# A graph network's first gather stage: transposes one slot ahead, a ring of ten slots, gathers unrolled

## What is computed

```
h    = concat([x[src], edge_attr], axis=1) @ W1 + b1      # 400000 x 64
mu, var = mean(h, axis=0), var(h, axis=0)                  # batch norm over all edges
msg  = silu((h - mu) * rsqrt(var + EPS) * g1 + be1)
agg  = segment_sum(msg, dst) / max(count(dst), 1)
```

## Time and profile before

| | |
|---|---|
| median of three runs | 10885.92 us (10885.71 to 10889.72) |
| the profiled execution's span, first to last instruction (no other time of it is given) | 10892.7 us |
| first gather stage, about 29 to 5072 us | 5043 us |
| between the gather stages | about 1150 us |
| second gather stage and the end | about 4670 us |
| busy share of the span: PE, DVE, ACT, POOL | 38%, 23%, 11%, 62% |
| granted TensorE clock, mean | 0.555 |

### The profile page before, as it was taken

How to read it: one execution, slowest core, us unless ns; L and a number is a source line. 1 busy time by engine, 2 the same in 40 slices (tenths; PEclk the granted TensorE clock), 3 DMA queues, 4 the chain that set the end, 5 groups by cost and what they waited for, 6 DMA issues and landing times. The chain is left out here.

```text
span 10892.7 us, 119855 instructions
## 1 busy us (share of the span) xinstructions
PE 4140.9 (38%) x36713; PEld 3322.5 (31%) x36713; DVE 2557.8 (23%) x7060; ACT 1173.7 (11%) x2055; POOL 6799.3 (62%) x6897
## 2 busy tenths in 40 slices
PE   4445444444444445445887311111111111111113
PEld 3333333333333333334776211111111111111112
DVE  2111111111111111114997311111111111111112
ACT  0000000000000000001334300000000000000001
POOL 5555555555555555556998466666666666666663
PEclk7655555656665655555555555555555555555555
DMA  2222222222222222222443111111111111111111
GB/s 78 60 61 61 61 61 60 61 61 61 61 61 61 61 60 61 61 61 75 125 123 114 50 44 44 43 45 44 44 44 44 44 43 45 44 43 45 44 44 35
DMA packets 882270, 637.83 MB, mean 59 GB/s; under 512 B 534579, under 2 KB 780831, under 8 KB 881496
## 3 DMA queue, kind: packets, MB, share of 16 engines
q1 hardware_dynamic: 590300, 326.49, 10.9%
q0 software_dynamic: 200416, 208.55, 10.2%
q10 hardware_dynamic: 91536, 102.58, 2.7%
HBM read 528.19 MB, written 108.90 MB: 58 GB/s over the span
## 5 line engine op out<-in xcount | busy, mean ns | idle before, releaser
L349 POOL DMA_INDIRECT Z<-in_x_dram,idx_ring x3125 | 2958.8, 947 | 2088.3 <-DVE idx_ring L526 1205.2
L1156 POOL DMA_INDIRECT X<-x_scratch,idx_ring x3125 | 2986.5, 956 | 1738.3 <-issue 893.5
L1185 PE MATMUL PS<-hot_c,msg_c 128*64 128x48 f32 x6250 | 811.6, 310 | 3865.8 <-ACT msg_c L1171 2630.0
L1185 PEld LDWEIGHTS PS<-hot_c,msg_c 128*64 128x64 f32 x6250 | 713.5, 223 | 3964.0 <-issue 2528.7
L401 PE MATMUL PS<-ZT,W_sb 128*64 128x256 f32 x2500 | 689.5, 647 | 2375.0 <-ACT ZT L451 2238.9
L515 DVE BATCH_NORM_STATS2 stats<-PS 128x320 f32 (+1 forms) x625 | 311.6, 499 | 3158.2 <-remote 2670.5
L1216 DVE TENSOR_TENSOR table<-table,PS 64x48 f32 x625 | 130.0, 208 | 3773.0 <-remote 1822.2
L401 PEld LDWEIGHTS PS<-ZT,W_sb 128*64 128x64 f32 x2500 | 183.7, 199 | 2637.2 <-ACT ZT L451 2488.9
L451 ACT ACTIVATE ZT<-PS 128x640 f32<-128x640 f32 x625 | 439.4, 703 | 4602.4 <-remote 4300.2
L391 PE MATMUL PS<-ident,Z 128*128 128x128 f32 x3125 | 845.7, 413 | 161.7 <-issue 158.6
L420 PE MATMUL PS<-W_sb,ZT 128*64 128x64 f32 x12500 | 877.7, 318 | 0.0
(11 more groups left out here) (140 smaller groups left out, 2682.9 us busy)
## 6 DMA issues: line engine op xcount, KB each, us to landing
Z<-in_edge_attr_dram SPq DMA_DIRECT2D x625, 160.0 KB
h_scratch<-h_ring ACTq DMA_DIRECT2D x625, 160.0 KB
h_turns<-h_scratch SPq DMA_DIRECT2D x125, 800.0 KB
E<-in_edge_attr_dram SPq DMA_DIRECT2D x625, 160.0 KB
Z<-in_x_dram,idx_ring POOLq DMA_INDIRECT x3125
X<-x_scratch,idx_ring POOLq DMA_INDIRECT x3125
x_nodes<-in_x_dram SPq DMA_DIRECT2D x1, 3125.0 KB
x_ring<-in_x_dram SPq DMA_DIRECT2D x25, 125.0 KB
```

The source lines that it names most:

```text
L349: nc.gpsimd.indirect_dma_start(out=Z[:, s, j, 0:D], out_offset=None, in_=x, in_offset=bass.IndirectOffsetOnAxis(ap=idx_ring[:, s, j:j + 1] ...
L1156: nc.gpsimd.indirect_dma_start(out=X[:, s, j, :], out_offset=None, in_=x1_dram, in_offset=bass.IndirectOffsetOnAxis(ap=idx_ring[:, s, j:j ...
L1185: last = nc.tensor.matmul(PS[D:P, s % 2, 0:WIN], msg[:, s, j, :], hot[:, s, j, :], start=(j == 0), stop=(j == TG - 1))
```

## The change

- PE transposes slot g+1 before the dense work of slot g. `ZT` has two buffers, taken by parity, so ACT's copy of slot g waits for the dense work of g-2.
- `Z`, `h_ring` and the one-hot have ten slots (RING = 2 S) in place of five. A turn has a half, 0 or 1, and the loops (`loop_halves`) run two turns a round.
- SP and POOL wait for the transposes of the slot ten back, with one counter `rows_done`. POOL's 3125 gathers are written out without a loop, and each takes its indices from a fixed column of `src_idx`; the copy into `idx_ring` (L526) and its signal are gone from this stage.
- DVE makes the one-hot of slot g+1 before it waits for slot g's results. ACT's store is that of two slots back.
- Several semaphores by slot become one counter each.

```diff
-            Z = sb(here, "Z", [P, S, TG, 2 * D])
-            ZT = sb(here, "ZT", [P, EG])
-            h_ring = sb(here, "h_ring", [P, S, TG, D])
+            RING = 2 * S
+            Z = sb(here, "Z", [P, RING, TG, 2 * D])
+            ZT = sb(here, "ZT", [P, 2, EG])
+            h_ring = sb(here, "h_ring", [P, RING, TG, D])
...
+            def later(i):
+                return not isinstance(i, int) or i >= 2
+
+            def next_slot(i, half, s, n):
+
+                return (i, half, s + 1, n) if s + 1 < S else (i + 1, 1 - half, 0, n + half)
...
+                            if later(i):
+                                sp.wait_ge(rows_done, i * S + (s + 1 - RING))
+                            sp.dma_start(Z[:, r, :, D:2 * D], edge_v[i * S + s]).then_inc(e_loaded[r], 16)
...
-                    def turn(i):
-                        for s in range(S):
-                            reuse(pool, idx_ready[s], i)
-                            reuse(pool, rows_done[s], i)
+                    for g in range(G):
+                        r = g % RING
+                        if g >= RING:
+                            pool.wait_ge(rows_done, g + 1 - RING)
                             carry_wait(pool)
-                            for j in range(TG):
-                                nc.gpsimd.indirect_dma_start(
-                                    out=Z[:, s, j, 0:D], out_offset=None, in_=x,
-                                    in_offset=bass.IndirectOffsetOnAxis(ap=idx_ring[:, s, j:j + 1], axis=0)
-                                ).then_inc(gathered[s], 16)
+                        for j in range(TG):
+                            n = g * TG + j
+                            nc.gpsimd.indirect_dma_start(
+                                out=Z[:, r, j, 0:D], out_offset=None, in_=x,
+                                in_offset=bass.IndirectOffsetOnAxis(ap=src_idx[:, n:n + 1], axis=0)
+                            ).then_inc(gathered[r], 16)
...
+                    def turn_rows(i, half, s, n):
+                        r = half * S + s
+                        if later(i) or i * S + s >= 2:
+                            pe.wait_ge(zt_taken, i * S + (s - 1))
+                        pe.wait_ge(e_loaded[r], n * 16 + 16)
+                        pe.wait_ge(gathered[r], n * (16 * TG) + 16 * TG)
...
+                        last.then_inc(rows_done, 1)
+
+                    def dense(i, half, s):
...
+                        pe.wait_ge(zt_taken, i * S + s + 1)
+                        if beyond:
+                            pe.wait_ge(count_added, i * S + (s - 1))
...
+                    def turn(i, half, n):
+                        for s in range(S):
+                            if not (isinstance(i, int) and i == SB - 1 and s == S - 1):
+                                turn_rows(*next_slot(i, half, s, n))
+                            dense(i, half, s)
...
+                            act.wait_ge(rows_done, i * S + s + 1)
+                            if later(i) or i * S + s >= 2:
+                                act.wait_ge(h_put, i * S + (s - 1))
+                            act.activation(ZT[:, two, :], banks(2 * two, 2, P, EG), ACT.Copy).then_inc(zt_taken, 1)
+                            if s >= 2:
+                                store(i, half, s - 2)
...
-                            nc.vector.tensor_copy(idx_ring[:, s, :],
-                                                  src_idx[:, ds(i * (S * TG) + (S + s) * TG, TG)]
-                                                  ).then_inc(idx_ready[s], 1)
+                            if not (isinstance(i, int) and i == SB - 1 and s == S - 1):
+                                one_hot(*next_slot(i, half, s, n))
+                            dve.wait_ge(ht_put, i * S + s + 1)
```

More of the change, by code:

```diff
@@ L313, in gnn_kernel @@
             h_put = sem("h_put")
-            h_ready = sems("h_ready")
-            h_stored = sems("h_stored")
+            h_ready = sem("h_ready")
+            h_stored = [sem(f"h_stored{r}") for r in range(RING)]
             stats_done = sem("stats_done")
@@ L379, in _ @@
                     pe.wait_ge(windows_ready, 1)
-                    def turn(i):
-                        for s in range(S):
[L383 to L418, removed]
-                                for lo in (0, D):
-                                    last = nc.tensor.matmul(PS[lo:lo + D, 6 + s % 2, j * D:(j + 1) * D],
-                                                            ZT[:, j * P + lo:j * P + lo + D], W1_sb[:, :],
-                                                            start=True, stop=True)
-                            last.then_inc(h_put, 1)
@@ L424, in _ @@
-                    turn(0)
-                    with pe.Fori(1, SB) as i:
-                        turn(i)
+                    def turn_rows(i, half, s, n):
+                        r = half * S + s
+                        if later(i) or i * S + s >= 2:
+                            pe.wait_ge(zt_taken, i * S + (s - 1))
+                        pe.wait_ge(e_loaded[r], n * 16 + 16)
+                        pe.wait_ge(gathered[r], n * (16 * TG) + 16 * TG)
+                        for j in range(TG):
+                            last = nc.tensor.transpose(banks(2 * (r % 2), 2, P, EG)[:, j * P:(j + 1) * P],
+                                                       Z[:, r, j, :], ident[:, :])
+                        last.then_inc(rows_done, 1)
@@ L457, in _, with store, turn @@
-                    turn(0)
-                    with act.Fori(1, SB) as i:
-                        turn(i)
-                    store(SB - 1, S - 1)
+                    def store(i, half, s):
+                        act.wait_ge(h_ready, i * S + s + 1)
+                        r = half * S + s
+                        act.dma_start(h_dram[i * S + s], h_ring[:, r, :, :].rearrange("p t c -> p (t c)")
+                                      ).then_inc(h_stored[r], 16)
+                    def turn(i, half, n):
+                        for s in range(S):
+                            two = (half * S + s) % 2
+                            act.wait_ge(rows_done, i * S + s + 1)
[4 more added lines that the diff above has]
+                                store(i, half, s - 2)
+                            elif not (isinstance(i, int) and i == 0):
+                                store(i - 1, 1 - half, s + S - 2)
@@ L530, in _ @@
-                    turn(0)
-                    with dve.Fori(1, SB) as i:
-                        turn(i)
+                            r = half * S + s
+                            two = r % 2
+                            if not (isinstance(i, int) and i == SB - 1 and s == S - 1):
+                                one_hot(*next_slot(i, half, s, n))
+                            dve.wait_ge(ht_put, i * S + s + 1)
+                            nc.vector.bn_stats(stats[:, ds(i * (6 * S) + 6 * s, 6)],
+                                               PS[:, 4 + two, 0:HC]).then_inc(stats_done, 1)
@@ new lines, in turn @@
+                            if not isinstance(i, int) or i * S + s > 0:
+                                dve.wait_ge(count_added, i * S + s)
+                            nc.vector.tensor_tensor(table[0:D, ds(firsts[s], WIN)], table[0:D, ds(firsts[s], WIN)],
+                                                    PS[0:D, 4 + two, HC:HC + WIN], ALU.add).then_inc(count_added, 1)
+                            dve.wait_ge(h_put, i * S + s + 1)
+                            if later(i):
+                                dve.wait_ge(h_stored[r], n * 16)
```

105 lines of the change are left out of this document (60 added, 45 removed).

## The result

The changed kernel took 10586.79 us (median of three runs, 10557.65 to 10588.93) against 10885.92 us: 0.9715 of the time before, 95% interval 0.9697 to 0.9732. That is 2.9% or 299 us faster. The forecast was 10452 us, 434 us faster. The profiled execution of after has a span of 10555.5 us and is the fastest of its three; that of before had 10892.7 us.

The account below looks back on a forecast made before the run. Gathers holding back TensorE's results, 1.41 to 1.43 us each, were taken as the bound. (8.05 - 7.35) x 620 slots = 434 us; 10892.7 - 434 - 7 = 10452 us; range 9960 to 10800 us, 8 times in 10.

Parts of the forecast that it names:

- Gathers hold back TensorE's results, 1.41 to 1.43 us each: Both gather stages: TensorE's results show late during gather trains, which makes 7.05 to 7.15 us a slot.
- The turn of 6.68 us: First gather stage: TensorE's time from one copy's end to the next copy, including some delay of the signal.
- The release: First gather stage: transposes of the slot ten back free gathers, so a train restarts about 3015.1 in place of 3016.03.
- The order on TensorE: First gather stage: transposing ahead takes the wait for the copy, 0.75 us a slot, off TensorE's path.
- slow bound: First gather stage: trains still of ten with the earlier restart, 7.63 us a slot.
- Trains longer than ten, with pauses left: First gather stage: 7.35 us a slot, taken between 7.1 and 7.63, saving 434 us over 620 slots.
- two bounds: First gather stage: quick bound 7.1 us a slot without pauses, slow bound 7.63 us with trains of ten.
- The start: Start of the first gather stage: the run-up's train of 50 gathers may delay the first slots by up to 15 us.
- Removed copy, longer queues, unrolled gathers: First gather stage: all costed at nothing; the unrolled gathers at most 0.55 us a slot.
- Full speed at 9770 us: Rival, first gather stage: trains hold nothing by themselves, gathers run at their pitch, 6.25 us a slot; chance 0.05.
- Slower: Rival, first gather stage: longer trains leave TensorE only the pauses, 8.8 us a slot, 11350 us; chance 0.11.
- the other stage has trains of 25 at 7.46 us a slot: Second gather stage: its shorter time a slot, despite longer trains, was held against the slower rival.

Follow-up runs that it names:

- gathers_3: The changed kernel with three gathers a slot, the other two tiles loaded by one plain DMA from SyncE; 8839.71 us, 0.8117 of the kernel before.
- pool_direct: The changed kernel with each gather replaced by a plain DMA of 128 rows from GpSimd's queue; 7508.97 us, 0.6896 of the kernel before.
- half_rows: The changed kernel with each gather fetching 64 rows, not 128, from the eleventh slot on; 10788.13 us, 0.9663 of the kernel before.
- order_back: The changed kernel with TensorE again transposing slot g right before the dense work of g; 11049.24 us, 0.9891 of the kernel before.
- h_two: The changed kernel with eight of the ten matmuls of h left out from the second turn on; 10455.41 us, 0.9593 of the kernel before.
- wide_h: The changed kernel with the ten matmuls of h as five of double width; 10733.12 us, 0.96 of the kernel before.
- after_again: The changed kernel itself, run again on the chip of the second group; 10582.0 us, 0.9717 of the kernel before.
- wide_fives: The changed kernel with five double-width matmuls of h, and GpSimd waiting once in five slots for five; 11695.52 us, 1.0494 of the kernel before.

## Why the forecast was right, and by how much it was off

- *Gathers hold back TensorE's results, 1.41 to 1.43 us each.* Right, and shown by taking gathers away and by changing the trains. With the train's length changed the figure stays: 1.45 (five), 1.44 (ten), 1.41 (fifteen), 1.42 (25), and (116.32 - 29.78) / 60 = 1.44 for the first train, of 60 gathers. With gathers left out a slot falls by 1.40 us each (gathers_3). It is the gather's indexed form, and by the instruction (pool_direct, half_rows). What the prediction saw as results that come to light late is also TensorE itself advancing in small steps. (The turn of 6.68 us that the prediction puts in the slot before the stalled one is that of the slot behind it; nothing hangs on this.)
- *The release: a train restarts 0.83 us after the copy, 15.25 us after its start.* Right: 0.77 us after it, 15.15 us after its start. With trains of ten on both sides this is 0.9 us for two slots, nearly all of the gain; but it needs the new order, without which the trains shorten to five.
- *The order on TensorE: 0.75 us a slot off its path.* This priced the wrong thing, and the forecast's sum left the order out. Without it the rest brings 1.1% only (order_back), for trains then have five gathers and pay the restart once a slot. That trains would stay at ten, as the slow bound supposes, hung on the order, and the prediction didn't see it: there the number is partly luck.
- *Trains longer than ten, with pauses left: 7.35 us a slot.* This is the term that was mis-sized, and it was chosen between two bounds, not worked out. Most trains stayed at ten (161 of 197), there were 662 gathers in 1000 us in place of 680, and a slot took 7.54 us over the stage, near the slow bound of 7.63. A slot costs 7.05 to 7.25 us for its five gathers, and 0.77 us divided by the slots in a train: 8.01, 7.58 and 7.33 us for one, two and three slots were measured. (8.05 - 7.54) x 620 = 316 us in place of 434. Trains of fifteen became common only with fewer instructions on TensorE (h_two, in part wide_h).
- *The start: up to 15 us.* Too low: 38 us, as a train of 60 gathers, not 50, holds the third slot. The end gives it back, since the last ten copies start behind the last gather's issue, at down to 2.15 us a slot. Net of both, 309 us by the last copies, of which 299 us show in the medians.
- *Removed copy, longer queues, unrolled gathers: nothing.* Right as far as seen: gather 0.95 us as before, one of over 3 us at the start in both kernels and no such stall every 25. The second gather stage, which is unchanged, takes 4651 us before and 4625 after from the first issue to the last (4648 in after_again); the windows of 4670 us before and 4772 after are not alike, for that of before leaves out the first 80 gathers. (The Trainium skill, Runtime: NRT & Kernel Launch, Instruction fetch mechanics, favours straight code; here the pitch of 1.25 us is the same with and without a loop.)
- *The rivals.* Full speed at 9770 us fell: trains hold by themselves, at a high clock too. At the stage's start before had a granted clock of 1.00 with gathers under way, and its fourth copy still came 10.39 us after the third had ended; a clock of 1.00 over a long stretch came only without gathers. "Slower" did not come, as far as seen because GpSimd still waits slot by slot; where it waits for five, it comes (1.0494). That the other stage has trains of 25 at 7.46 us a slot, which the prediction held against this rival, was no argument: it has far less work on TensorE.

Open: why an indexed gather holds TensorE. The steps of 0.7 us would fit two holds a gather, since 2 x 0.7 is the 1.4, but no run tests this, and no row says by what TensorE is held, nor which part of its work (its instructions, its operands or its signals) it is. Open too is whether a pitch truly above 1.41 us would free TensorE.

## What to carry to other kernels

Count indirect gathers as a price on TensorE, here 1.4 us an instruction for 64 rows as for 128, beside their price on GpSimd; the way on is fewer of them, or plain DMAs where the rows allow it. Here a slot without gathers took 2.15 us in place of 7.55. If gathers come in trains, what can be tuned is how often the restart is paid: let the signal that frees a gather be the earliest possible, and order TensorE so that two or three slots are freed at once. Don't force longer trains: TensorE does little inside one, and its backlog comes out as idle time of GpSimd (9.1 us a slot with trains of 25).

## What was not expected of the hardware

- TensorE's records deep in a train start in steps of about 0.7 us with one to five short matmuls in each: 0.37 us of work every 2.10 us in wide_fives.
- A gather of 64 rows holds TensorE 1.47 us, one of 128 rows 1.44 us; a plain DMA of 128 rows from GpSimd takes 0.53 us of GpSimd and holds nothing that shows.
- Another chip took 2.6% longer for the kernel before (11169.67 against 10885.92 us). Of these 284 us, some 170 would lie in the second gather stage, as an estimate from the traces of the changed kernels on that chip (about 4820 us from first to last issue against 4651); before has no trace there. Ratios of like kernels shifted by some 0.7% with it (0.9644 and 0.9717 at 660 and 662 gathers in 1000 us).
